# Graph attention layers: one gathered chunk of 32 moves from GpSimd to SyncE

## The reference

```python
h = (x @ W).reshape(n, heads, -1)
al_s = jnp.einsum('nhf,hf->nh', h, a_src)
al_d = jnp.einsum('nhf,hf->nh', h, a_dst)
e = jax.nn.leaky_relu(al_s[src] + al_d[dst], NEG_SLOPE)
m = jax.lax.stop_gradient(jax.ops.segment_max(e, dst, num_segments=n))
ex = jnp.exp(e - m[dst])
denom = jax.ops.segment_sum(ex, dst, num_segments=n)
alpha = ex / (denom[dst] + 1e-16)
out = jax.ops.segment_sum(h[src] * alpha[:, :, None], dst, num_segments=n)
```

## Time and profile before

| | |
|---|---|
| Median of 3 executions | 5352.69 us (5352.2 to 5355.13) |
| The profiled execution | 5359.02 us, its span 5356.7 us |
| Busy over the span | PE 3603.2 us (67%), DVE 3488.2 (65%), POOL 3415.3 (64%), PEld 2236.0 (42%), ACT 1434.4 (27%) |
| Instructions | 76877 |
| Mean granted clock of TensorE | 0.759 |
| DMA | 663.55 MB, 124 GB/s in the mean |

### The profile page before, as it was taken

How to read it: one execution, slowest core, us unless ns; L and a number is a source line. 1 busy time by engine, 2 the same in 40 slices (tenths; PEclk the granted TensorE clock), 3 DMA queues, 4 the chain that set the end, 5 groups by cost and what they waited for, 6 DMA issues and landing times. The chain is left out here.

```text
span 5356.7 us, 76877 instructions
## 1 busy us (share of the span) xinstructions
PE 3603.2 (67%) x12542; PEld 2236.0 (42%) x12543; DVE 3488.2 (65%) x8997; ACT 1434.4 (27%) x3112; POOL 3415.3 (64%) x3722
## 2 busy tenths in 40 slices
PE   3477777777777777646777777777777774139980
PEld 2244444444444444424444444444444443127760
DVE  5677777777777777666767767677677676414434
ACT  1222223223222232243222222222222222112220
POOL 2477777777777777536777777777777771441117
PEclk9777777777777777777777777777777775569995
DMA  3344444444444444335444444444445444222216
GB/s 90 103 133 132 133 132 132 134 132 132 133 132 134 132 132 134 92 142 152 132 131 131 133 131 131 132 131 133 131 131 133 131 127 161 70 74 65 64 58 188
DMA packets 306626, 663.55 MB, mean 124 GB/s; under 512 B 77231, under 2 KB 134239, under 8 KB 306298
## 3 DMA queue, kind: packets, MB, share of 16 engines
q0 software_dynamic: 178288, 488.60, 33.4%
q1 hardware_dynamic: 114590, 156.59, 10.5%
q10 hardware_dynamic: 13708, 17.94, 0.9%
HBM read 596.01 MB, written 68.42 MB: 124 GB/s over the span
## 5 line engine op out<-in xcount | busy, mean ns | idle before, releaser
L882 POOL DMA_INDIRECT rows<-table,idx x3232 | 3058.5, 946 | 1051.8 <-issue 914.6
L955 PE MATMUL bank<-rows,hit 128*128 128x260 f32 (+1 forms) x6464 | 2620.5, 550 | 1062.5 <-DVE acc L1017 1056.0
L955 PEld LDWEIGHTS bank<-rows,hit 128*128 128x128 f32 x6464 | 1472.6, 256 | 2007.2 <-DVE acc L1017 1767.2
L1017 DVE TENSOR_TENSOR acc<-acc,bank 128x260 f32 (+1 forms) x3232 | 1350.2, 418 | 175.9 <-issue 29.0
L1008 DVE TENSOR_TENSOR rows<-rows,bank 128x1024 f32<-128x1024 f32 x808 | 945.0, 1210 | 1.5 <-ACT rows L915 1.5
L912 ACT ACTIVATE arg<-arg 128x32 f32<-128x32 f32 (+1 forms) x404 | 89.2, 221 | 2820.3 <-DVE arg L1001 2820.3
L994 DVE TENSOR_TENSOR arg<-rows,bank 128x32 f32<-128x32 f32 (+1 forms) x404 | 71.4, 177 | 990.1 <-DMA rows<-table,idx 990.1
L975 DVE TENSOR_TENSOR hit<-bank,dst_loc 128x256 f32<-128x256 f32 x1616 | 668.7, 415 | 0.1
L944 PE MATMUL bank<-du,hit_t 128*128 x3232 | 376.2, 184 | 162.7 <-ACT hit_t L906 123.5
L901 ACT ACTIVATE gap<-loc,minus_node 128x1024 bf16<-128x1024 bf16 x404 | 463.7, 1148 | 52.2 <-DMA loc<-loc_row 52.0
L906 ACT ACTIVATE hit_t<-gap,ones 128x1024 bf16<-128x1024 bf16 x404 | 465.1, 1151 | 20.7
(11 more groups left out here) (187 smaller groups left out, 1980.2 us busy)
## 6 DMA issues: line engine op xcount, KB each, us to landing
loc<-loc_row SPq DMA_DIRECT2D x404, 256.0 KB, 3.5
rows<-table,idx POOLq DMA_INDIRECT x3232
sent<-zeros SPq DMA_DIRECT2D x1, 13568.0 KB, 47.8
xe<-sent SPq DMA_DIRECT2D x106, 128.0 KB, 2.0
back<-ye POOLq DMA_DIRECT2D x106, 128.0 KB, 2.0
fw<-in_L_ffn_W ACTq DMA_DIRECT2D x16, 512.0 KB, 10.5
table<-acc POOLq DMA_DIRECT2D x49, 130.0 KB, 2.3
table<-acc POOLq DMA_DIRECT2D x49, 128.5 KB, 2.4
```

The costliest lines, as they stand in the source:

```text
L882: pool.indirect_dma_start(rows[:, way, n, 0:R], None, table, bass.IndirectOffsetOnAxis(idx[:, way, n:n + 1], 0)).then_inc(rows_in[way], 16)
L955: nc.tensor.matmul(sum_bank[n % 4][:, 0:R], hit[:, way, n, :], rows[:, way, n, 0:R], start=True, stop=True).then_inc(summed, 1)
L1017: nc.vector.tensor_tensor(kp.acc[:, t, 0:R], kp.acc[:, t, 0:R], sum_bank[n % 4][:, 0:R], ALU.add).then_inc(added, 1)
```

## The change

In both layers, the last chunk of the fourth step of every group of four (step 3, 7, ...) is no longer gathered by GpSimd. SyncE fetches its 128 rows by 128 DMAs of one row each, 32 in each of the group's four steps. It loads 32 row numbers into registers at a time (`sp.load`), and each DMA takes its source address from one of them. The row numbers come from `sp_idx`, loaded from a new table `src_row` in memory, which the preparation phase writes. The rows land in two buffers of their own, `sp_rows`, used in turn. ScalarE copies the chunk's source terms from there into `rows` (`copy_sp_term`) before it makes the weights of that step; VectorE multiplies the other chunks of the half step in place and this one from `sp_rows` into `rows`. All loops of the phase are repeated for eight ways now (TURN). The last two steps of a layer (200 and 201) are gathered as before. So 50 chunks per layer change hands. The core of the diff:

```diff
+    BATCH = 32
+    TURN = 2 * SETS
+    BY_SP = (SETS - 1, ST - 1)
...
+                regs = [sp.alloc_register(f"sp_row{m}_{layer}") for m in range(BATCH)]
...
+                def load_idx(half, turn):
+                    item = (turn * TURN + half * SETS + BY_SP[0]) * ST + BY_SP[1]
+                    sp.dma_start(sp_idx[:, half, :], kp.src_row[bass.ds(item, 1), :]).then_inc(sp_idx_in[half], 16)
...
+                def gather_rows(half, quarter, turn):
+                    sp.load(regs, sp_idx[0:1, half, quarter * BATCH:(quarter + 1) * BATCH])
+                    for m in range(BATCH):
+                        n = quarter * BATCH + m
+                        if n == P - 1:
+                            wait_idx(1 - half, turn + half)
+                        row = sp.snap(regs[m], min_val=0, max_val=N - 1)
+                        sp.dma_start(sp_rows[n:n + 1, half, 0:R], table[bass.ds(row, 1), :]
+                                     ).then_inc(sp_rows_in[half][quarter // 2], 16)
+
+                def step(s, way, turn):
+                    load(s, way, turn)
+                    half, quarter = way // SETS, way % SETS
+                    if not number(s) or s // SETS < STEPS // SETS:
+                        gather_rows(half, quarter, turn)
+                    if quarter == SETS - 1 and (not number(s) or s + 1 + 2 * SETS <= STEPS):
+                        load_idx(half, turn + 1)
...
                     for n in range(ST):
+                        if (way % SETS, n) == BY_SP:
+                            continue
...
+                def copy_sp_term(s, half, turn):
+
+                    for q in range(2):
+                        act.wait_ge(sp_rows_in[half][q], (turn + 1) * (2 * 16 * BATCH))
+                    if not number(s) or s >= SETS:
+                        act.wait_ge(summed, (s - SETS + 1) * ST)
+                    nc.scalar.copy(rows[:, BY_SP[0], BY_SP[1], D:D + H], sp_rows[:, half, D:D + H]
+                                   ).then_inc(sp_term, 1)
...
-                    nc.vector.tensor_tensor(
-                        r, r, weight[:, some, :].unsqueeze(3).to_broadcast([P, PIECE, H, D // H]), ALU.mult
-                    ).then_inc(scaled, 1)
+                    done = nc.vector.tensor_tensor(
+                        r, r, weight[:, some, :].unsqueeze(3).to_broadcast([P, PIECE - by_sp, H, D // H]), ALU.mult)
+                    if by_sp:
+                        done = nc.vector.tensor_tensor(
+                            rows[:, way, ST - 1, 0:D].rearrange("p (h f) -> p h f", h=H),
+                            sp_rows[:, half, 0:D].rearrange("p (h f) -> p h f", h=H),
+                            weight[:, ST - 1, :].unsqueeze(2).to_broadcast([P, H, D // H]), ALU.mult)
+                    done.then_inc(scaled, 1)
```

More of the change, by code:

```diff
@@ L125, in build @@
         keep.loc_row = dram("loc_row", [BLOCKS * P, W], BF16)
+        keep.src_row = dram("src_row", [BLOCKS * P, W], I32)
         keep.tile_row = dram("tile_row", [BLOCKS, P], I32)
@@ L239, in plan_phase @@
         loc_written = b.sem("loc_written")
+        src_written = [b.sem(f"src_written{j}") for j in range(2)]
         rows = WROWS // SPLIT
@@ L823, in edge_phase @@
         arg = b.sb(f"arg_{layer}", [P, 2, ST, H], F32)
+        sp_idx = b.sb(f"sp_idx_{layer}", [1, 2, P], I32)
+        sp_rows = b.sb(f"sp_rows_{layer}", [P, 2, D + HEADS], F32)
+        sp_idx_in = [b.sem(f"sp_idx_in{half}_{layer}") for half in range(2)]
+        sp_rows_in = [[b.sem(f"sp_rows_in{half}{q}_{layer}") for q in range(2)] for half in range(2)]
+        sp_term = b.sem(f"sp_term_copied_{layer}")
         idx_ready = b.sem(f"idx_ready_{layer}")
@@ L859, in load, with wait_idx @@
                     step_rows = kp.loc_row[bass.ds(s * ST, ST), :]
-                    sp.dma_start(loc[:, way, :], step_rows.rearrange("i w -> (i w)").unsqueeze(0).to_broadcast(
-                        [P, ST * P])).then_inc(loc_in[way], 16)
-                steps(sp, STEPS, load)
+                    sp.dma_start(loc[:, way % 2, :], step_rows.rearrange("i w -> (i w)").unsqueeze(0).to_broadcast(
+                        [P, ST * P])).then_inc(loc_in[way % 2], 16)
+                def load_idx(half, turn):
+                    item = (turn * TURN + half * SETS + BY_SP[0]) * ST + BY_SP[1]
+                    sp.dma_start(sp_idx[:, half, :], kp.src_row[bass.ds(item, 1), :]).then_inc(sp_idx_in[half], 16)
+                def wait_idx(half, turn):
+                    if not number(turn) or turn * TURN + half * SETS + SETS <= STEPS:
+                        sp.wait_ge(sp_idx_in[half], (turn + 1) * 16)
+                def gather_rows(half, quarter, turn):
[14 more added lines that the diff above has]
+                        load_idx(half, turn + 1)
+                load_idx(0, 0)
+                load_idx(1, 0)
+                wait_idx(0, 0)
+                steps(sp, STEPS, step, TURN)
                 if clear is not None:
@@ L881, in gather @@
                     for n in range(ST):
[L882 to L886, removed]
+                        if (way % SETS, n) == BY_SP:
+                            continue
+                        pool.indirect_dma_start(rows[:, way % SETS, n, 0:R], None, table,
+                                                bass.IndirectOffsetOnAxis(idx[:, way % SETS, n:n + 1], 0)).then_inc(
+                                                    rows_in[way % SETS], 16)
+                steps(pool, STEPS, gather, TURN)
             @block.scalar
@@ L918, in step @@
                     if not number(s) or s + 3 < STEPS:
-                        stage(s + 3, (way + 3) % SETS, turn + (way + 3) // SETS)
+                        stage(s + 3, (way + 3) % TURN, turn + (way + 3) // TURN)
                     if not number(s) or s + 2 < STEPS:
-                        make_hit_t(s + 2, (way + 2) % SETS, turn * 2 + (way + 2) // 2)
+                        make_hit_t(s + 2, way % 2, turn * SETS + (way + 2) // 2)
                     if not number(s) or s + 1 < STEPS:
-                        weigh(s + 1, (way + 1) % SETS)
+                        if (way + 1) % SETS == BY_SP[0]:
+                            copy_sp_term(s + 1, way // SETS, turn)
+                        weigh(s + 1, way + 1)
                 for first in range(3):
@@ L929, in _ @@
                 weigh(0, 0)
-                steps(act, STEPS, step, SETS)
+                steps(act, STEPS, step, TURN)
             @block.tensor
@@ L958, in step @@
                 def step(s, way, turn):
-                    sum_rows(s, way, range(0, 4))
+                    sum_rows(s, way % SETS, range(0, 4))
                     if not number(s) or s + 2 < STEPS:
                         spread_du(s + 2, (way + 2) % SETS)
-                    sum_rows(s, way, range(4, ST))
+                    sum_rows(s, way % SETS, range(4, ST))
                 spread_du(0, 0)
                 spread_du(1, 1)
-                steps(pe, STEPS, step, SETS)
+                steps(pe, STEPS, step, TURN)
             @block.vector
@@ L1064, in _ @@
                 for piece in range(PIECES):
-                    scale_rows(0, 0, piece)
-                steps(dve, STEPS, step, SETS)
+                    scale_rows(0, 0, piece, 0)
+                steps(dve, STEPS, step, TURN)
                 dve.load(t_regs, eb.tile_of[0:1, bass.ds((STEPS - 1) * ST, ST)])
```

27 lines of the change are left out of this document (20 added, 7 removed).

## The result

| | before | after |
|---|---|---|
| device time, median | 5353.91 us (5352.2 to 5355.46) | 8097.64 us (8096.13 to 8099.47) |
| profiled span | 5356.7 us | 8094.5 us |
| edge phase, first gather to last addition, layer 1 / layer 2 | 2040.8 / 2064.5 us | 3386.8 / 3435.1 us |
| first gather of layer 1 starts at | 210.9 us | 231.1 us |

The changed kernel takes 1.5125 times as long (95% interval 1.5099 to 1.5151), 352 us more than the 7745 predicted and inside the range of 6600 to 8400. Both edge phases grow by two thirds, the rest of the program only by 20 us at its start.

A forecast was written before the change was run, and what follows sets the result against it. GpSimd's gather issue bounds the kernel; afterwards SyncE would, at 63.0 us per group. 5359.0 + 1146 (layer 1) + 1172 (layer 2) + 5 (preparation) + 70 (jumps) = 7752, so 7745 us as median; range 6600 to 8400.

The forecast's parts named there:

- four loads of loc: SyncE's stream, once per step: 0.54 us each from register work, DMA and gaps, 2.1 us per group.
- indices, loop and jump: Rest of SyncE's group: indices 0.4 us, loop and waits 0.3; the loop's jump was counted separately, 70 us in total.
- The row: One row fetch on SyncE: FUSED_REGOPS 54, MOVE 29, DMA 218 and gaps 120 ns, taken as 0.42 us; bounds 0.26 to 0.62.
- register work hidden: Rival of cheaper rows: register work runs behind the DMA, a row costs 0.26 to 0.285 us, total 5695 to 6015; 7%.
- The register load: SyncE's load of 32 row numbers: 1.6 us with its gap, 6.4 us per group; bounds 0.59 and 2.4 us each.
- The jump: End of SyncE's long loop, 23 times per layer: 46 x 0 to 3.0 us, 0 to 138, taken as 70 us.
- The preparation: Before the edge phases: 13 more DMAs of about 0.37 us on SyncE, +5 us (0 to 15).
- The named wait: Sign in the profile after: ScalarE's long wait before the copy of the term, on a DMA into sp_rows.
- What the edit buys: On GpSimd: one of 32 gathers less in each of 100 groups, 125 us if nothing else became late.
- SyncE keeps up: Faster side case: a row under 0.231 us leaves GpSimd the bound, gain 125 us less 5 and small waits, 5235 us; 3%.

The follow-up runs named there:

- fixed rows: Changed kernel with its 128 one-row DMAs per group from addresses fixed in the program, no register work before a row; register loads were gone too: 5582.44 us.
- disturbed round: Round of runs on a disturbed chip, in which the kernel before itself took 6510 us in nine runs; nothing was read from it and its runs were repeated.
- one register load for all: Changed kernel with one load of 32 registers ahead of the loop instead of 400, each row's register work kept: 8598.56 us first, 7280.57 us when run again.

## Why the prediction was right, and what it sized wrong

Right in its mechanism: SyncE becomes the bound, it runs at its own speed, all others wait for it, and the total follows the group time at 100 us per us. One group of SyncE's stream, in us:

| term | forecast | measured | difference |
|---|---|---|---|
| 128 rows, short halts between instructions included | 53.8 | 54.7 | +0.9 |
| four register loads | 6.4 | 8.4 | +2.0 |
| four loads of loc | 2.1 | 2.3 | +0.2 |
| indices, loop and jump | 1.4 | 1.9 | +0.5 |
| group | 63.7 | 67.25 | +3.6 |

The phases of layer 1 and 2 took 3386.8 and 3435.1 us where 3223 and 3271 had been forecast, jumps included: 164 more in each. With 15 in the preparation and some 10 between the profiled executions and the medians that is the miss of 352. 100 x 3.6 would be 360 and not 328, because the table shows a group inside the loop; the first and last turns of a layer stand outside it, have no jump, and take 65 to 66 us per group.

- **The row** is right to 1%: 0.419 for 0.42 us, with some luck. FUSED_REGOPS is 44 and not 54 ns, the DMA 228 and not 218, and the two errors cancel. That MOVE comes with every row of a register address was read from one line; without it (0.35 us) the forecast would have been some 900 us lower, with the register work hidden (0.26 to 0.285) 2,100 to 2,400 us below what was measured. The fixed rows show what this work is worth: 0.295 in place of 0.419 us.
- **The register load** is the largest mis-sized term. 40 ns for each further register was taken from 1 and 8 registers on TensorE's sequencer. On SyncE 16 registers take 1166 and 32 take 2057 ns: 56 ns each. A slope between two short loads of another sequencer was carried to four times its length. It lies inside the bound of 2.4 us, which took 73 ns for each. The page "Runtime: NRT & Kernel Launch" of the Trainium skill gives about 200 ns per register under Instruction fetch mechanics, for a TENSOR_LOAD that it describes elsewhere as a load from HBM. These loads, from a tile on the core, cost 64 ns per register, all included, so that figure does not hold for them.
- **The jump** came out near the upper end of 0 to 3.0 us, 2.4 to 3.1 each, 114 us in all where 70 had been put. Not priced were short halts of about 0.3 us within the body, some six per turn, included in the first line of the table. The instruction queue carries 650 packets where it carried 29; 261 come also where GpSimd gathers into the new buffers, with the other engines' loops doubled and SyncE's short, so some 390 are SyncE's. The trace agrees with the rule of the same page and section of the Trainium skill that a taken branch to code outside the window brings a fetch.
- **The preparation** was put at +5 (0 to 15) and costs 20. The writes of src_row were counted as issue time of SyncE; what matters is the buffer that they keep from GpSimd, and that SyncE starts them only at 40 us.
- **The named wait** was wrong in one point: ScalarE's long wait was expected before the copy, for sp_rows, and stands before gap, for loc. The loads of loc stand between the row fetches in the same queue, so each of them is late first. With loc moved away, the expected wait appears.
- **What the edit buys** was right: the one DMA in place of 32 gave 64.5 and 60.0 us for 62.6, and the side case "SyncE keeps up", 5235 us, was met by 5259. Of the 24 us 18 are the preparation, which had been put at 5, and 6 the slower kernel before of that round.

## What to carry to other kernels

An engine that the profile shows idle is not free for small DMAs: write down its instruction stream for one period, register work, gaps, loads and jump included, and compare it with the period of the bound. One gather of 128 rows costs GpSimd 1.25 us here, the same rows one by one cost SyncE 54 us, so of the two shares tried one chunk in 64 gained and one in 32 lost. When several things come late from one queue, the waits name the last one only; moving it away moves the wait and shows the real bound.

## What the runs showed of the hardware

- The jump of one and the same loop can cost 0.3 or 2.7 us. With fixed rows, the timeline of SyncE shows first a turn's end in layer 1, then one in layer 2:

```profile
1547.47 0.24 SPq L883 DMA_DIRECT2D sp_idx<-src_row  x1
1548.36 0.37 SPq L878 DMA_DIRECT2D loc<-loc_row  x1
...
3428.23 0.23 SPq L883 DMA_DIRECT2D sp_idx<-src_row  x1
3431.47 0.38 SPq L878 DMA_DIRECT2D loc<-loc_row  x1
```

 From the index load to loc's it is 0.89 us in one and 3.24 in the other, for the same instructions at another place of the program. The instruction queue tells them apart. Its packets in 1000 us of layer 1 (400 to 1400), then of layer 2 (2800 to 3800):

```profile
q14 instruction: 60, 0.49, 0.2%
...
q14 instruction: 117, 0.96, 0.3%
```

 That is 5 packets per turn in layer 1 and 10 in layer 2; where GpSimd gathers into the new buffers and SyncE's loop is short, they are 63 and 63, 5 per turn as well. So SyncE's long jump goes with fetches of code, and the short one does without. What in the placement decides it was not tested.

- A DMA of one row takes SyncE 252 ns when it stands back to back and 228 with register work between.
- In the disturbed round SyncE's stream halted for about 0.7 us at a time, between its instructions and inside them. SyncE's MOVEs before the rows in the first run of one register load for all, where the longest was 37 ns in the second:

```profile
L895 SPq MOVE sp_rows<-table x12800: 1/29/1453, 237.0 to 7627.1; - x197
```

 It did not halt all streams, as one expectation says: register instructions of over 0.5 us stand on SyncE (158 in 1500 us of that run) and a few on VectorE (2), none on the other engines. The kernel before lost 21% there, and has no trace of that round. The cause stays open.
